# First attention: the low parts of W2 subtracted on GpSimd instead of VectorE

## What is computed

```python
x = x + L0_xattn(layernorm(x), ctx)      # 16 heads of 16, 77 keys
x = x + L0_ffn(layernorm(x))             # W1 256x1024, sine transform, relu, W2 1024x256
x = x + L1_xattn(ctx, layernorm(x), mask)
x = x + L1_ffn(layernorm(x))             # blockwise fp4 of inputs and weights, 704 wide
```

## Time and profile before

| | |
|---|---|
| median of 3 runs | 926.62 us |
| the runs | 925.99 to 928.49 us |
| the profiled execution's own time | 927.38 us |
| its span, first to last instruction | 925.6 us |
| mean granted TensorE clock | 0.993 of full speed |
| busy: TensorE, VectorE, ScalarE, GpSimd | 885.8, 779.7, 522.2, 459.8 us |

### The profile page before, as it was taken

How to read it: one execution, slowest core, us unless ns; L and a number is a source line. 1 busy time by engine, 2 the same in 40 slices (tenths; PEclk the granted TensorE clock), 3 DMA queues, 4 the chain that set the end, 5 groups by cost and what they waited for, 6 DMA issues and landing times.

```text
span 925.6 us, 20182 instructions
## 1 busy us (share of the span) xinstructions
PE 885.8 (96%) x7216; PEld 797.3 (86%) x7216; DVE 779.7 (84%) x2117; ACT 522.2 (56%) x1147; POOL 459.8 (50%) x661
## 2 busy tenths in 40 slices
PE   7899999999899999999899999998879999999998
PEld 5799999998799999988899999997758888888886
DVE  6999999999677777755999999997868898989886
ACT  3534343434688888886665656564644544444443
POOL 2233433342566677745224333432247777777772
PEclk9999999999999999999999999998989999999999
DMA  9120000000000000001000000000000000000001
GB/s 328 72 104 2 2 2 1 2 2 1 2 1 1 1 1 2 1 1 56 1 2 2 1 2 2 2 2 1 1 1 1 24 24 24 1 24 23 24 1 46
DMA packets 6515, 18.31 MB, mean 20 GB/s; under 512 B 912, under 2 KB 3344, under 8 KB 5904
## 3 DMA queue, kind: packets, MB, share of 16 engines
q1 hardware_dynamic: 5552, 16.65, 4.7%
q10 hardware_dynamic: 864, 0.37, 0.2%
HBM read 12.83 MB, written 4.19 MB: 18 GB/s over the span
## 4 chain that ended last, share of the span: by engine, by line
PE 70%; DVE 10%; ACT 9%; POOL 6%; issue 3%; DMA 1%; ACTq 0%; POOLq 0%; DVEq 0%
PE a_psO L1230 14%; PE s_psY L1448 10%; PE s_psH L1437 9%; PE f_psGU L1941 7%; PE a_psQ L1192 6%; PE a_psT L1219 6%; PE a_psS L1171 5%; PE f_psY L1933 5%; ACT a_qTs L1116 3%; ACT a_prob L1099 3%; POOL f_hval L1772 2%; PE a_psQ L1180 2%; POOL f_hres L1778 2%; PE a_psY L1180 1%; DVE f_hid L1609 1%
## 5 line engine op out<-in xcount | busy, mean ns | idle before, releaser
L1230 PE MATMUL a_psO<-vblk,a_prob 128*128 128x51 f32 (+1 forms) x1280 | 148.4, 271 | 0.0
L1230 PEld LDWEIGHTS a_psO<-vblk,a_prob 128*128 128x128 f32 x1280 | 148.0, 192 | 0.0
L1941 PE MATMUL f_psGU<-late_wgu,f_xTs 128*128 128x512 f32 (+1 forms) x576 | 141.4, 390 | 6.3 <-ACT late_wdT L1874 3.2
L950 DVE TENSOR_REDUCE a_mx<-a_psS 128x4 f32<-128x308 f32 x256 | 115.2, 471 | 9.2 <-PE a_psS L1171 3.9
L1941 PEld LDWEIGHTS f_psGU<-late_wgu,f_xTs 128*128 128x128 f32 x576 | 104.0, 192 | 21.2 <-ACT late_wdT L1874 3.4
L1099 ACT ACTIVATE a_prob<-a_psT 128x512 f32<-128x512 f32 (+1 forms) x192 | 101.8, 530 | 23.7 <-PE a_psT L1219 22.6
L958 DVE TENSOR_TENSOR a_shifted<-a_psS,a_mx 128x308 f32<-128x308 f32 x256 | 114.8, 469 | 0.0
L1219 PE MATMUL a_psT<-ident,a_shifted 128*128 128x128 f32 x640 | 106.2, 281 | 8.3 <-ACT a_prob L1099 5.0
L1087 ACT COPY a_xTs<-a_psQ 128x256 f32<-128x256 f32 x64 | 23.9, 373 | 159.8 <-PE a_psQ L1180 159.6
L1448 PEld LDWEIGHTS s_psY<-e_w,s_hid 128*128 128x128 f32 x768 | 100.1, 188 | 8.7 <-POOL s_hid L1368 3.5
L1368 POOL TENSOR_TENSOR s_hid<-s_full,s_hid 128x512 fp32r<-128x512 f32 x64 | 82.9, 1296 | 45.8 <-ACT s_full L1403 45.8
(11 more groups left out here) (193 smaller groups left out, 1830.3 us busy)
## 6 DMA issues: line engine op xcount, KB each, us to landing
out_x<-x SPq DMA_DIRECT2D x7, 512.0 KB, 2.6
x<-in_x SPq DMA_DIRECT2D x3, 1024.0 KB, 16.0
w<-in_w SPq DMA_DIRECT2D x1, 2304.0 KB, 8.7
w<-in_w SPq DMA_DIRECT2D x2, 1024.0 KB, 13.8
a_mask<-in_mask SPq DMA_DIRECT2D x4, 308.0 KB, 3.8
wat<-in_att SPq DMA_DIRECT2D x1, 1024.0 KB, 15.2
x<-in_x SPq DMA_DIRECT2D x1, 768.0 KB, 10.5
wat<-in_att SPq DMA_DIRECT2D x2, 256.0 KB, 4.9
```

The source lines that it names most:

```text
L950: nc.vector.tensor_reduce(mx[:, u, j * BH:(j + 1) * BH], psS[j][:, 0:BH * KV].rearrange("p (h k) -> p h k", k=KV), AX.X, ALU.max).then_inc ...
L1230: mm = nc.tensor.matmul(psO[:, CH[c] * VW:(CH[c] + n) * VW], prob[:, u, c * P:(c + 1) * P], vblk[:, t // R, c * NJ * VW:(c * NJ + n) * VW] ...
L1941: mm = nc.tensor.matmul(psGU[:, n0:n1], xTs[:, u, a, k * P:(k + 1) * P], wgu[:, b, k, n0:n1], start=(n == 0), stop=(n == len(TERMS) - 1))
```

## The change

The low parts of quarters 2 and 3 (both halves of W2) are made by GpSimd, at the end of the deviation and bias work of its step 3, with the same `tensor_tensor` subtraction on the same operands. The low parts of quarters 0 and 1 stay on VectorE, the high parts on ScalarE. GpSimd's instruction waits for w_high and counts w_split as VectorE's did; SyncE's wait for four counts is as before.

```diff
     src, high, low = w_quarter(g, n)
     dve.wait_ge(g["w_high"], n + 1)
-    if n < 2:
-        nc.vector.scalar_tensor_tensor(low, src, TURNS, high.bitcast(F32), ALU.mult, ALU.subtract
-                                       ).then_inc(g["w_split"], 1)
-    else:
-        nc.vector.tensor_tensor(low, src, high.bitcast(F32), ALU.subtract).then_inc(g["w_split"], 1)
+    nc.vector.scalar_tensor_tensor(low, src, TURNS, high.bitcast(F32), ALU.mult, ALU.subtract
+                                   ).then_inc(g["w_split"], 1)
+
+
+def w_low_on_gpsimd(nc, pool, g, n):
+
+    src, high, low = w_quarter(g, n)
+    pool.wait_ge(g["w_high"], n + 1)
+    nc.gpsimd.tensor_tensor(low, src, high.bitcast(F32), ALU.subtract).then_inc(g["w_split"], 1)
...
             for n in self.quarters_of(i):
-                w_low_parts(nc, dve, g, n)
+                if n < 2:
+                    w_low_parts(nc, dve, g, n)
...
             if valid(i + 2):
                 add_bias(i + 2)
+            for n in self.quarters_of(i):
+                if n >= 2:
+                    w_low_on_gpsimd(nc, pool, g, n)
             if piece_of(i - 1) is not None:
                 w4_rounding(nc, pool, g, piece_of(i - 1), piece_of(i - 1) % 2)
```

## The result

Over 22 runs of each, the changed kernel takes 929.13 us in the median (925.84 to 933.63), the kernel before 927.21 (925.93 to 930.73): a ratio of 1.0019, 95% interval 1.001 to 1.0028, that is +1.8 us with an interval of 0.9 to 2.6. The forecast was +1.07 us, 927.7; the time lies in the range of 925.8 to 929.8, and within 0.3% of before. The profiled execution took 929.55 us, its span is 927.7, its mean granted clock 0.989 where before had 0.993.

A forecast was written before the change was run, and what follows sets the result against it. TensorE sets the pace, with VectorE close behind. Removing the subtractions gives 0, the late load adds +1.07 us; against the median of 926.62 that makes 927.7 us, range 925.8 to 929.8.

The forecast's parts named there:

- What is removed: VectorE's two subtractions in step 3, 2.33 us, covered by TensorE's weighted-value products: gain 0, bounds 0 and -0.1 us.
- Rival (b): VectorE was the bound in step 3, so at most 1.65 us come back: 925.0 us; chance 0.02.
- The pair: The two subtractions on GpSimd at the end of its step 3: 2.43 us each, 4.86 together.
- The load: Next weights into w4, issued at 51.20 and landing at 59.90, so VectorE stands still 1.31 us in step 5.
- Rival (a): The load stays hidden if the pair takes at most 3.8 us: 926.6 us; chance 0.12.
- From the wait to the time: Of VectorE's 1.31 us wait, 0.24 is free; TensorE's step 6 pays +1.07 us, kept to the end.
- the wait less 0.24: Lateness of on(4), input of the attended transposes: 0.24 us is free, the rest lengthens step 6 one for one.
- its own definition of a step: The distance between two starts of TensorE's score products in the first attention; regular length 6.62 us.
- (d), the clock: TensorE's half-clock stretches at the switch to the last stage, one more or fewer: plus or minus 1.6 us; chance 0.07.
- slower rival (c): Pair of 6.4 us or more, later load, GpSimd colliding with VectorE's normalise in step 4: +2.9 us, 929.5; chance 0.04.

The follow-up runs named there:

- two later comparisons: The unedited changed kernel measured again, a second and a third time, against the kernel before: ratios 1.0007 and 1.0004.
- first comparison: The changed kernel against the kernel before, 22 runs of each: 929.13 against 927.21 us in the median, ratio 1.0019.

## Why the prediction was right, and where it was off

**What is removed: right.** It forecast no gain and an idle VectorE until the weighted values; 2.08 us of idleness stand there, and steps 3 and 4 keep their length. Rival (b) is out.

**The pair: right, a little high.** 4.86 forecast, 4.70 measured (2.35 each). The slope between 256 and 512 elements carried over to 1024. The estimate of 4.5 us by the rate in the Trainium skill, page GPSIMD Engine Reference, section Elementwise — side-by-side cycle accounting, is 0.2 too low.

**The load: the right mechanism, the wait too long.** 1.31 us forecast, 0.81 to 1.06 measured. In the profile after, the difference of 0.45 is 0.16 of the pair, 0.2 of the load's time (8.5 for 8.7) and 0.08 of a VectorE that comes to the load later in its step. Rival (a), the hidden load, is out in this form, and near: one quarter on GpSimd is that case.

**From the wait to the time: right in the sum, not in its place.** The rule "the wait less 0.24" gives 0.62, 0.67, 0.61, 0.57, 0.78 and 0.79 us for the waits of 0.86, 0.91, 0.85, 0.81, 1.02 and 1.03. Wherever the clock stayed full, steps 5 and 6 grew by 0.66, 0.62, 0.59, 0.77 and 0.77 (each sum less 13.76, in the order 0.91, 0.85, 0.81, 1.02, 1.03); in the changed kernel's first profile, step 6 without the half clock would be 7.06 as in the others, which makes 0.62. The prediction had put all of it on step 6 (about 7.7) and left step 5 at 7.14, although it also let step 6's scores start 0.5 us late, which by its own definition of a step lengthens step 5. Measured, step 5 grows by the wait less 0.66 to 0.69 us, so the queries had about 0.68 us to spare and not 0.83, and step 6 grows by 0.44 whatever the wait. (Where GpSimd subtracts three times, the held normalise comes on top of that in step 5.)

**What was wrong: (d), the clock.** The prediction said that these stretches lie at the switch to the last stage, gave a difference of 1.6 us or more 0.07, and put the clock at nothing in its sum. They also come at 31, at 62, at 236 and at 457 us, in some executions: 9 of the 14 profiles have one before 600 us. One near 62 us cost 8.63 - 7.06 = 1.57 us, the size that the prediction gave (1.6). So the profiled execution's +2.19 in two steps are 0.62 of waiting and 1.57 of clock. How much of the clock's part belongs to the change can be read from many runs: in the two later comparisons the mean granted clock of the changed kernel is 0.9917 and 0.9914, of the kernel before 0.9916 and 0.9917, no difference that their standard error, 0.0008, would show. Among runs with the same 0.993, the changed kernel takes 927.99 and 927.59 us, the kernel before 927.18 and 927.19: +0.8 and +0.4, in line with the direct part. Among those with 0.991 the difference is +0.9 and +0.3, among the few with 0.989 it is -0.1 and +0.1. In the first comparison, with +1.8 us, the changed kernel's mean clock was 0.9907; how before's stood there is not recorded. The later two ratios, 1.0007 and 1.0004, lie under the first, and their intervals meet it. The direct cost of 0.6 to 0.8 us is shown in the steps; that the rest of the +1.8 comes from stretches that this set of runs happened to have more of is likely and not proven.

**The slower rival (c)** did not happen, and its lock was shown to be real in the kernel that keeps GpSimd busy 2.4 us longer. It was priced at 0.3 us for a pair of 6.4; three subtractions, 7.1 us, paid 0.8. One argument against it was too wide: it held every operation with one operand of SBUF to be safe, and the normalise, which reads x alone as a tensor, was held.

**What was luck.** The direct cost was forecast at 1.07 us and is 0.62 in the profile after, since the load was forecast to be later than it was. That the measured +1.8 lies on the other side of the forecast comes from something the sum had at nothing, likely the clock. The two errors pull in opposite directions. Of the 1.4 us between the forecast of 927.7 and the median of 929.13, 0.6 is the kernel before itself, whose median was 926.62 in 3 runs and 927.21 in 22.

## What to carry to other kernels

An operation moved off a busy engine gains nothing if that engine would then only wait for the one that sets the pace: look at what ended its next idle time before counting the microseconds. Then follow the signal of the moved operation: here a transfer that reuses the tile had 2.85 us of margin, the move used up about 3.7, and the part beyond came back as a stall on the very engine that was to be relieved. Where a tile is released in parts, loading it in parts removed this dependence here at no cost in time that could be measured (ratio 0.9994).

## What the runs showed of the hardware

GpSimd subtracts 128x1024 in 2.35 us where VectorE takes 1.2. Some of VectorE's operations on SBUF alone are held to the end of an operation of GpSimd that started earlier: a normalise by 0.82 us, a tensor_scalar or a two-input operation on 8 elements by 0.42; bn_stats was not. The reverse holds too: VectorE's subtraction held GpSimd's deviation (1.08 us for 0.19). Not every such pair of operations is held: before, VectorE's two-input operations on 8 elements at 53.29 and 53.49 took 0.17 us each beside GpSimd's one-column operation (53.23, 0.55). The operations that read PSUM kept their length all through GpSimd's 4.70 us. TensorE was granted 1.2 GHz for some 3.4 us at a time at places that differ from execution to execution of one program; with the execution time between 925.84 and 933.63 us, this is most of the scatter: in the runs of one chip the kernel before took 927.12 us on average at a mean clock of 0.993, 928.47 at 0.991 and 929.81 at 0.989.
